# Chunked attention with a low-rank MLP on eight cores: layernorm sums ahead of the k means, the variance on ScalarE alone, and the U1 product inside attention

## What is computed

```python
xn = layernorm(x, eps=1e-5)
# attention: 16 heads of 64, chunks of 128 positions (64 chunks)
q, k, v = xn @ wq.T + bq, xn @ wk.T + bk, xn @ wv.T + bv
intra = softmax(q @ k.T / 8) @ v                 # inside a chunk, all positions
k_means, v_means = k.mean(chunk), v.mean(chunk)  # one row a chunk
inter = softmax(q @ k_means.T / 8, chunks up to its own) @ v_means
attn = (intra + inter) @ wo.T + bo
# MLP of rank 256, 4096 wide
P = xn @ U1; H = gelu_tanh(P @ V1 + b1); Q = H @ U2
mlp = Q @ V2 + b2
out = x + attn + mlp
```

## Time and profile before

| | us |
|---|---|
| timed runs (2) | 3545.97 and 3664.36, median 3605.16 |
| profiled execution, time | 3525.01 |
| its span, slowest core | 3523.5 (eight cores: 3516.6 to 3523.5) |
| mean granted TensorE clock, eight cores | 0.787 to 0.789 |
| busy in the span: TensorE matmuls | 2402.8 (68%) |
| ScalarE | 1197.8 (34%) |
| VectorE | 1078.0 (31%) |
| GpSimd | 298.0 (8%) |

### The profile page before, as it was taken

One profiled execution on the slowest core, in us unless ns is written; L12 is line 12 of the kernel. 1 busy time (PEld: TensorE's weight loads), 2 busy tenths in 40 slices (PEclk: granted clock), 3 DMA queues, 4 the chain that ended last, 5 costly groups with the idle time before them and its releaser, 6 DMA issues.

```text
span 3523.5 us, 41273 instructions; the slowest of 8 cores (3516.6 to 3523.5 us)
## 1 busy us (share of the span) xinstructions
PE 2402.8 (68%) x14259; PEld 1144.9 (32%) x14403; DVE 1078.0 (31%) x2572; ACT 1197.8 (34%) x2080; POOL 298.0 (8%) x558
## 2 busy tenths in 40 slices
PE   1267858676786767758576785866668576785867
PEld 0223333332333233333332333333333323333333
DVE  2432241423314232241423224142331423324141
ACT  0025143342524334243332514334252333514333
POOL 1101010100101010010100101010010101001010
PEclk9986959688695977959687695968869587695968
DMA  7500101001010100101000010100101010010000
GB/s 118 87 1 2 48 3 48 2 13 36 3 48 3 48 2 8 43 2 48 3 26 23 2 48 3 48 2 13 36 3 48 3 42 8 2 48 3 24 2 25
DMA packets 45431, 86.06 MB, mean 24 GB/s; under 512 B 17292, under 2 KB 24108, under 8 KB 44972
## 3 DMA queue, kind: packets, MB, share of 16 engines
q1 hardware_dynamic: 18348, 67.24, 5.3%
q0 software_dynamic: 26880, 16.18, 3.4%
HBM read 62.03 MB, written 34.60 MB: 27 GB/s over the span
## 4 chain that ended last, share of the span: by engine, by line
PE 54%; DVE 22%; issue 9%; ACT 4%; DMA 4%; POOL 2%; DVEq 1%; ACTq 0%; POOLq 0%
PE B L421 13%; PE B L893 7%; PE B L440 7%; PE B L863 7%; PE B L839 6%; DVE kcol L467 4%; DVE z L551 3%; PE B L684 3%; DVE km_fm L472 2%; DVE out_st L917 2%; DVE stats L341 2%; PE B L674 2%; PE B L748 2%; DMA lse_scr<-rows_cd 2%; PE B L903 2%
## 5 line engine op out<-in xcount | busy, mean ns | idle before, releaser
L839 PE MATMUL B<-P_fm,V 128*128 128x512 bf16 x1008 | 318.2, 405 | 200.4 <-DVE P_fm L826 199.6
L847 ACT ACTIVATE H_rot<-B,b_f 128x512 bf16<-128x512 f32 x512 | 348.2, 687 | 89.7 <-PE B L839 88.9
L430 ACT ACTIVATE q_fm<-B,bq_eff 128x512 bf16<-128x512 f32 x128 | 87.9, 687 | 725.9 <-PE B L421 725.9
L893 PE MATMUL B<-woT,attn_fm 128*128 128x512 bf16 x992 | 239.8, 378 | 136.9 <-DVE out_st L917 110.5
L863 PE MATMUL B<-H_rot,U 128*128 128x512 bf16 x1008 | 304.4, 385 | 10.8 <-ACT H_rot L847 8.9
L454 DVE CAST v_tm<-B 128x512 bf16<-128x512 f32 x128 | 88.6, 692 | 676.1 <-PE B L448 676.1
L421 PE MATMUL B<-xn_fm,wqT 128*128 128x512 bf16 x992 | 249.3, 415 | 37.7 <-DVE xn_fm L405 36.9
L684 PE MATMUL B<-H_rot,ones 2*128 2x512 bf16 x256 | 153.1, 598 | 149.0 <-DMA H_rot<-lse_scr 94.1
L440 PE MATMUL B<-wvT,xn_fm 128*128 128x512 bf16 x1008 | 242.2, 380 | 0.8
L617 PE MATMUL B<-identity,neglse 128*32 128x128 f32 x64 | 24.1, 377 | 314.8 <-DVE neglse L609 314.8
L421 PE MATMUL B<-xn_fm,wkT 128*128 128x512 bf16 x1008 | 222.8, 379 | 0.8
(11 more groups left out here) (106 smaller groups left out, 3171.7 us busy)
## 6 DMA issues: line engine op xcount, KB each, us to landing
x_buf<-L_attn_hidden_states SPq DMA_DIRECT2D x16, 2048.0 KB, 10.2
out<-out_st SPq DMA_DIRECT2D x64, 512.0 KB, 2.6
V<-L_ffn_V POOLq DMA_DIRECT2D x1, 2048.0 KB, 24.4
U<-L_ffn_U POOLq DMA_DIRECT2D x1, 2048.0 KB, 40.4
H_rot<-L_attn_wq POOLq DMA_DIRECT2D x8, 256.0 KB, 4.0
H_rot<-L_attn_wk POOLq DMA_DIRECT2D x8, 256.0 KB, 3.8
H_rot<-L_attn_wv POOLq DMA_DIRECT2D x8, 256.0 KB, 4.0
H_rot<-L_attn_wo POOLq DMA_DIRECT2D x8, 256.0 KB, 3.9
```

Of the source, the lines that this page charges most:

```text
L839: pm.do("t", (lambda bk=bk, g=g, rc=rc: lambda e: e.matmul(B[bk][:], V1[:, rc * 4096 + g * 128:rc * 4096 + g * 128 + 128], P_fm[:, rc * 51 ...
L847: pm.do("s", (lambda bk=bk, g=g: lambda e: e.activation(H_rot[:, (g % 4) * 512:(g % 4) * 512 + 512], B[bk][:], AF.Gelu_apprx_tanh, bias=b1 ...
L893: e.matmul(B[bk][:], attn_fm[:, ec * 512 + st * 128: ec * 512 + st * 128 + 128], woT[:, ec * 1024 + half * 512: ec * 1024 + half * 512 + 512],
```

## The change

- A new `emit_ln_sums(scx)` makes, for the four tiles, the sum and the negative mean on VectorE. For the next stage it is called right after the v projection, ahead of the k means.
- `emit_ln` no longer has these, nor the square of the mean and the variance step. Square now takes the negative mean as its per-partition bias, so that its accumulator is the sum of squared deviations, and Ln takes 1/1024 as a scale from a new column of `cvals`. All Squares wait for the sums of all four tiles.
- The U1 product and the copies to `P_fm` move from behind attention and layernorm to behind the lse bounce of chunk 0, and take their banks from the pool.
- As `P_fm` is now written within attention, the flat buffer of odd chunks moves to `Q_fm`.

```diff
@@ constants, flat buffers @@
+    cv[:, 6] = 1.0 / 1024
-                 1: (H_rot[32:34, 0:2048], P_fm[0:4, 0:1024])}
+                 1: (H_rot[32:34, 0:2048], Q_fm[0:4, 0:1024])}
@@ layernorm @@
-    def emit_ln(scx):
+    def emit_ln_sums(scx):
+        parx = scx % 2
+        xbx = x_buf[:, parx * 4096:(parx + 1) * 4096]
+        for st in range(4):
+            xt = xbx[:, st * 1024:(st + 1) * 1024]
+            s_sum = stats[:, st * 4:st * 4 + 1]
+            s_nm = stats[:, st * 4 + 2:st * 4 + 3]
+            pm.do("v", (lambda xt=xt, s_sum=s_sum: lambda e:
+                        e.reduce_sum(s_sum, xt, axis=AX.X))(),
+                  waits=[d_xp[parx], x_guard[parx], c_v.snap()], incs=[(c_v, 1)])
+            pm.do("v", (lambda s_sum=s_sum, s_nm=s_nm: lambda e:
+                        e.tensor_scalar(s_nm, s_sum, -1.0 / 1024, None,
+                                        ALU.mult))(),
+                  waits=[c_v], incs=[(c_v, 1)])
+        return c_v.n
+
+    def emit_ln(scx, sums_v):
-            w0 = [d_xp[parx], kq_guard]
-            pm.do("v", (lambda xt=xt, s_sum=s_sum: lambda e:
-                        e.reduce_sum(s_sum, xt, axis=AX.X))(),
-                  waits=w0 + [x_guard[parx], c_v.snap()], incs=[(c_v, 1)])
-            pm.do("s", (lambda xt=xt, xnt=xnt, s_sq=s_sq: lambda e:
-                        e.activation(xnt, xt, AF.Square, accum_out=s_sq))(),
-                  waits=w0 + [x_guard[parx], c_s.snap()], incs=[(c_s, 1)])
-            pm.do("v", (lambda s_sum=s_sum, s_nm=s_nm: lambda e:
-                        e.tensor_scalar(s_nm, s_sum, -1.0 / 1024, None, ALU.mult))(),
-                  waits=sw + [c_v.snap()], incs=[(c_v, 1)])
-            pm.do("v", (lambda s_sq=s_sq, s_nm=s_nm: lambda e:
-                        e.tensor_tensor(kcol[:], s_nm, s_nm, ALU.mult))(),
-                  waits=[c_v], incs=[(c_v, 1)])
-            pm.do("v", (lambda s_sq=s_sq: lambda e:
-                        e.tensor_scalar(s_sq, s_sq, 1.0 / 1024, kcol[:, 0:1],
-                                        ALU.mult, ALU.subtract))(),
-                  waits=[c_v], incs=[(c_v, 1)])
+            pm.do("s", (lambda xt=xt, xnt=xnt, s_sq=s_sq, s_nm=s_nm: lambda e:
+                        e.activation(xnt, xt, AF.Square, bias=s_nm,
+                                     accum_out=s_sq))(),
+                  waits=[(c_v, sums_v), kq_guard, c_s.snap()], incs=[(c_s, 1)])
             pm.do("s", (lambda s_sq=s_sq, s_rs=s_rs: lambda e:
-                        e.activation(s_rs, s_sq, AF.Ln, bias=cvals[:, 0:1]))(),
-                  waits=vw, incs=[(c_s, 1)])
+                        e.activation(s_rs, s_sq, AF.Ln, bias=cvals[:, 0:1],
+                                     scale=cvals[:, 6:7]))(),
+                  waits=[c_s], incs=[(c_s, 1)])
@@ behind the v projection, ahead of the k means @@
+        if sc + 1 < nsc:
+            ln_sums_next = emit_ln_sums(sc + 1)
@@ attention and U1: the rc loop now stands ahead of the cc loop @@
         nl0 = emit_p1(0)
         fl0 = emit_lse_bounce(0, nl0)
         flat_v = {0: fl0}
-        for cc in range(4):
-            ...
-        if sc + 1 < nsc:
-            ln_next = emit_ln(sc + 1)
-
         for rc in range(2):
-            bk = rc
+            bk = pool_next()
             ...
-        p_done = c_v.n
+        p_done_sc = c_v.n
+        for cc in range(4):
+            ...
+        if sc + 1 < nsc:
+            ln_next = emit_ln(sc + 1, ln_sums_next)
+
+        p_done = p_done_sc
```

More of the change, by code:

```diff
@@ L334, in emit_ln @@
             xnt = xn_tm[:, st * 1024:(st + 1) * 1024]
-            w0 = [d_xp[parx], kq_guard]
-            s_sum = stats[:, st * 4:st * 4 + 1]
             s_sq = stats[:, st * 4 + 1:st * 4 + 2]
@@ L339, in emit_ln @@
             s_rs = stats[:, st * 4 + 3:st * 4 + 4]
-            pm.do("v", (lambda xt=xt, s_sum=s_sum: lambda e:
-                        e.reduce_sum(s_sum, xt, axis=AX.X))(),
-                  waits=w0 + [x_guard[parx], c_v.snap()], incs=[(c_v, 1)])
-            pm.do("s", (lambda xt=xt, xnt=xnt, s_sq=s_sq: lambda e:
-                        e.activation(xnt, xt, AF.Square, accum_out=s_sq))(),
-                  waits=w0 + [x_guard[parx], c_s.snap()], incs=[(c_s, 1)])
-            sw = [c_s.snap()]
-            pm.do("v", (lambda s_sum=s_sum, s_nm=s_nm: lambda e:
-                        e.tensor_scalar(s_nm, s_sum, -1.0 / 1024, None, ALU.mult))(),
-                  waits=sw + [c_v.snap()], incs=[(c_v, 1)])
-            pm.do("v", (lambda s_sq=s_sq, s_nm=s_nm: lambda e:
-                        e.tensor_tensor(kcol[:], s_nm, s_nm, ALU.mult))(),
-                  waits=[c_v], incs=[(c_v, 1)])
-            pm.do("v", (lambda s_sq=s_sq: lambda e:
-                        e.tensor_scalar(s_sq, s_sq, 1.0 / 1024, kcol[:, 0:1],
-                                        ALU.mult, ALU.subtract))(),
-                  waits=[c_v], incs=[(c_v, 1)])
-            vw = [c_v.snap()]
+            pm.do("s", (lambda xt=xt, xnt=xnt, s_sq=s_sq, s_nm=s_nm: lambda e:
+                        e.activation(xnt, xt, AF.Square, bias=s_nm,
+                                     accum_out=s_sq))(),
+                  waits=[(c_v, sums_v), kq_guard, c_s.snap()], incs=[(c_s, 1)])
             pm.do("s", (lambda s_sq=s_sq, s_rs=s_rs: lambda e:
-                        e.activation(s_rs, s_sq, AF.Ln, bias=cvals[:, 0:1]))(),
-                  waits=vw, incs=[(c_s, 1)])
+                        e.activation(s_rs, s_sq, AF.Ln, bias=cvals[:, 0:1],
+                                     scale=cvals[:, 6:7]))(),
+                  waits=[c_s], incs=[(c_s, 1)])
             pm.do("s", (lambda s_rs=s_rs: lambda e:
@@ L365, in emit_ln @@
             pm.do("v", (lambda xt=xt, xnt=xnt, s_nm=s_nm, s_rs=s_rs: lambda e:
-                        e.tensor_scalar(xnt, xt, s_nm, s_rs, ALU.add, ALU.mult))(),
-                  waits=sw2, incs=[(c_v, 1)])
+                        e.tensor_scalar(xnt, xt, s_nm, s_rs, ALU.add,
+                                        ALU.mult))(),
+                  waits=sw2 + [c_v.snap()], incs=[(c_v, 1)])
             ln_done.append(c_v.n)
         return ln_done
-    ln_next = emit_ln(0)
+    ln_next = emit_ln(0, emit_ln_sums(0))
     for sc in range(nsc):
@@ L796, in build_nc @@
         flat_v = {0: fl0}
-        for cc in range(4):
[L798 to L805, removed]
-        a_guard = (c_t, av_done_prev[0])
-        attn_done_v = c_v.n
-        kq_guard = (c_t, c_t.n)
-        if sc + 1 < nsc:
-            ln_next = emit_ln(sc + 1)
         for rc in range(2):
-            bk = rc
+            bk = pool_next()
             w = [(c_v, xn_ready), bank_free[bk]]
@@ L828, in build_nc @@
             bank_free[bk] = (c_v, c_v.n)
-        p_done = c_v.n
+        p_done_sc = c_v.n
+        for cc in range(4):
+            if cc + 1 < 4:
+                nl = emit_p1(cc + 1)
+            exp_done_st[0] = {}
+            emit_p2_av(cc, flat_v[cc], 0)
+            if cc + 1 < 4:
+                flat_v[cc + 1] = emit_lse_bounce(cc + 1, nl)
+            emit_p2_av(cc, flat_v[cc], 1)
+            emit_p2_av(cc, flat_v[cc], 2)
+        a_guard = (c_t, av_done_prev[0])
+        attn_done_v = c_v.n
+        kq_guard = (c_t, c_t.n)
+        if sc + 1 < nsc:
+            ln_next = emit_ln(sc + 1, ln_sums_next)
+        p_done = p_done_sc
         xnfm_guard = (c_t, c_t.n)
```

## The result

The changed kernel is slower by 0.26%: 3536.45 us median (3531.4 to 3692.7, 43 runs) against 3527.4 us (3523.4 to 3719.8, 42 runs), ratio 1.0026, 95% interval 1.0014 to 1.0039, that is some 9 us. By the mark of 2% that is no change, as forecast; but the interval leaves out 1, so the small loss is real, and I had forecast -0.2 us. The time lies in the stated range.

What follows compares the result with a forecast made beforehand. No engine bounds throughout; the kernel is a relay of stages. Terms +6.4 - 10.4 + 2.4 + 1.7 = +0.1 us, times 15 = +1.5, stage 15 -2.3, start +0.6: -0.2 on 3525, so 3525 us; range 3503 to 3575, 8 in 10 3470 to 3600.

Steps and rivals of the forecast that it cites:

- the two places: In each stage: TensorE's wait for P_fm, some 12.5 us; VectorE's 32 k-means pairs before the first z sum, on the path.
- parts 1 and 2: Sums ahead of the k means, +6.4 us a stage; layernorm on ScalarE alone, earlier gelu table load, -10.4 us a stage.
- part 5: Flat buffer in Q_fm instead of P_fm and bank rotation by two: same transfers, no effect.
- Part 3: U1 and P_fm copies in attention's chunk 0: 5.5 us less 3.1 us of TensorE slack, +2.4 us a stage.
- Part 4: U2 starts at the low clock after TensorE's wait for the gelu: +1.7 us a stage.
- The start: First layernorm: the sums of all four tiles precede the first Square, +0.6 us.
- Stage 15: Last stage, without layernorm: table load 5.5 us earlier, against 2.4 for U1 and some 0.8 for the clock, -2.3 us.
- Warm attention: Rival: after U1 the clock stays at 2.4 GHz through attention, -6.7 us a stage, 3425 us; chance 0.13.
- U1 wholly on the path: Rival: no slack in chunk 0, U1 costs attention 8.2 us instead of 2.4, 3612 us; chance 0.10.
- The drain: Rival: about 1.38 us of drain at the gelu table load directly behind an Exp, 3546 us; chance 0.07.
- The stretch at 1427.5: Evidence against the clock staying up: from 1427.5 to 1433.2 TensorE was busy 2.57 of 5.7 us and the clock fell.

Runs made afterwards that it cites:

- e8: The changed kernel with U1's 16 matmuls made twice in attention; ratio 1.0193 to the kernel before.
- e5: The changed kernel with 28 extra unread matmuls on TensorE while it waits for the gelu ahead of U2; ratio 0.9985 to the kernel before.
- e9: The changed kernel with 40 extra unread matmuls on TensorE while it waits for the gelu ahead of U2; ratio 0.9938 to the kernel before.
- e1: The changed kernel run again, unaltered, for an undisturbed trace; ratio 1.0027 to the kernel before.
- e3: The changed kernel with U1 and its P_fm copies back behind the layernorm; ratio 0.9997 to the kernel before.
- e7: The changed kernel with sums ahead of the v copies, U1 right behind the v product, and Square, Ln, Exp ahead of it; ratio 0.923 to the kernel before.
- e4: The kernel before with only U1 and the P_fm copies moved into attention, flat buffer in Q_fm; ratio 1.0049 to the kernel before.

## Why the prediction was right or wrong

| term, us | forecast | measured |
|---|---|---|
| 1 sums, per stage | +6.4 | +6.39 |
| 2 layernorm on ScalarE | -10.4 | -10.47 |
| 3 U1 in attention | +2.4 | +2.74 (1.6 to 3.3) |
| 4 clock at U2 | +1.7 | +1.47 |
| first gelu to first U2 | 0 | +0.22 |
| other stretches | 0 | +0.22 |
| stages 0 to 14 | 15 x 0.1 = +1.5 | 15 x 0.57 = +8.5, projections -1.9 |
| stage 15 | -2.3 | -0.1 |
| start | +0.6 | +2.2 |
| sum | -0.2 | +8.9 |

*Reading the two places and their bound* was right, and so were parts 1 and 2, to a tenth; of part 5 nothing is to be seen. The cost of a pointer operand held: Square 1.15 us against 1.06.

*Part 3* had the right mechanism and was too small by a seventh. The clock stayed at 0.50 for U1's first 5.1 us in the mean rather than the 4 or so of my middle value, and U1 lasts 6.2 us (6.4 in stage 6) instead of 5.5. The slack of 3.1 us in chunk 0 was as read: in stage 6, 6.3 (1512.57 to 1518.88) less 3.1 is 3.2, and the second transpose moved by 2.9; chunk 1's scores now began at full clock (the first group of L542 takes 0.62 us, 1.03 before), which is about what is missing. e8 shows that beyond it all counts.

*Part 4* was right in kind and near in size, and e5 and e9 show the cause. U2 stood at 0.50 for 4.1 us in the mean, as I took it; but before, U2 had lost 0.6 us a stage to the clock rather than 0.4.

*The step that failed* is the last of the working, "In all -0.2 us": its terms were too rough for the sign that it gave. Per stage it is the difference of two terms of 10 us, and over 15 stages 0.4 us a stage decide the sign. The term that was mis-sized most is part 3, U1 in attention: +2.4 forecast, +2.74 measured, some 5 us in 15 stages. Two terms stood at nothing without a reason: 0.22 between the first gelu and U2 and 0.22 in small stretches, 3.3 us each. Part 4 and the projections gave some 5 back. I gave the sum as the center and took "no change" for the answer, though these omissions leaned to the slow side. Its own range, 3503 to 3575, held.

*The start* had a gap too, +0.6 forecast and +2.2 measured. The setup ends alike: the first layernorm sum starts at 163.27 before and at 163.09 now. From there to the last of the four normalizations it was 14.5 us before and is 16.5 now, on all eight cores. Of these 2 us, 1.28 are ScalarE's first table load. Before, it was done during the setup, since the first Square waited for no sum; now it is held back with that Square until the four sums are there. The rest is the 0.6 that I had counted.

```profile
150.98 1.28 ACT L344 ACT_TABLE_LOAD   x1 [150.98 <-PEq L275]
...
169.40 1.28 ACT L356 ACT_TABLE_LOAD   x1 [169.40 <-DVE stats L340]
```

(The first line is of before, the second of e1.)

*Stage 15* is off by 2.2 us on the core of the table, and this is in part chance of that core. The table load came 5.9 us earlier (forecast 5.5), but U1 cost 3.7 there instead of 2.4, and U2, which before started warm behind a dense U1, was 1.83 us longer, not 0.8. On four of the cores 0 to 5 of that execution (0, 2, 3 and 4) U2 of stage 15 took its old 26.82 us, and over these six cores stage 15 changed by -0.3 to -3.0 us against the same core of before, 1.7 in the mean. The forecast, -2.3, lies within.

The 0.22 from gelu to U2 is open. It is absent before and in e3, where U1 stands right behind attention, and there in all the others; the clock is not its cause, as e7 has it too with U2 at full clock.

*The rivals.* Warm attention (0.13) did not come: the clock rose in U1, stayed at 1.00 for some 6.8 us in 15 of 16 stages and fell ahead of chunk 0's second pass. The Trainium skill, "TensorE: Matmul & The Clock Gate", section on why this matters for your kernels, ties the fall to gaps between bursts; here it fell with waits of 0.7 and 2.6 us in a stretch where TensorE was busy 3.8 of 6.5 us. The stretch at 1427.5 of the earlier trace rows, which spoke against that rival, was the better guide. U1 wholly on the path (0.10) is refuted by e1 and e4. The drain (0.07) did not appear: in e1 the gelu table load starts at 1574.69, at once behind the last Exp, and U2 begins 2.35 us after it, against 2.12 in the earlier trace rows; the difference is the 0.22 above. The Trainium skill, "ScalarE: Activation LUTs", section on what ACT_TABLE_LOAD costs, gives a duration that agrees (1.28 us here) and a drain that neither this load nor that of the earlier trace rows shows.

## What to carry to other kernels

Moving work ahead of its deadline gains only if it lands in idle time of its engine: the same four sums cost 95 us behind the v copies and nothing ahead of them. Before pricing what a move takes away, look at what the next waiting engine has in its own queue; the wait for `P_fm` was 12.5 us long, but only 3.4 us came back when it went (e4), because ScalarE's share of the layernorm ended just before it. Where a forecast is the small difference of large terms, give it a sign only if the left-out terms are known to be smaller, and say that it has none otherwise.

## What the runs showed of the hardware

Filling TensorE's wait with 40 matmuls whose product nobody reads made a kernel 0.9% faster, since the stretch behind it began at 2.4 GHz instead of 1.2. With 28 of them a wait was left ahead of that stretch: in the five of fifteen stages where it was 2.9 to 3.2 us long the clock fell within a microsecond of U2's start, in the ten with 1.8 to 2.6 us it did not.

Sixteen dense matmuls in the middle of attention raised the clock, but the attention work behind them did not hold it: it fell after some 6.8 us, and stayed at 1.2 GHz through 40.5 us in which TensorE was busy for 32.9.

One reduction over 8 x 128 elements took 1.22 us, eight of 128 elements took 2.3 us of busy time, and 5.2 us with their scalings and the hand-overs between them.

An activation table load began right behind the operation before it, at 1574.69 where that ended at 1574.68, and the gelu right behind the load, at 1575.99 where that ended at 1575.97.
